# Sparse-coding kernel: coefficients scattered by index through DRAM in place of one-hot rows, sums and transposes

## The reference, cut to what matters

```python
D = dictionary / (norm(dictionary, axis=0) + EPS)      # 512 x 256
h_bar = (D.T @ X).T                                    # per patch: 256 scores
for k in range(1, 6):
    index = argmax(abs(h * ~mask))                     # one atom a step
    ...                                                # solve for x_stack (k coefficients)
    h = h_bar - einsum('bk,bkn->bn', x_stack, G[I])    # G = D.T @ D + eps
coeffs = zeros((B, N)).at[bidx[:, None], I].set(x_stack)
x = x1 + from_patches(D @ coeffs.T)
```

## Time and profile before

| | |
|---|---|
| median of 3 runs | 619.07 us (617.48 to 621.41) |
| the profiled execution | 618.9 us, of it 616.8 us from the first to the last instruction |
| VectorE busy | 523.9 us (85%) |
| TensorE busy | 459.3 us (74%) |
| ScalarE busy | 310.9 us (50%) |
| GpSimd busy | 222.6 us (36%) |
| mean granted TensorE clock | 0.902 of full speed |

### The profile page before, as it was taken

How to read it: one execution, slowest core, us unless ns; L and a number is a source line. 1 busy time by engine, 2 the same in 40 slices (tenths; PEclk the granted TensorE clock), 3 DMA queues, 4 the chain that set the end, 5 groups by cost and what they waited for, 6 DMA issues and landing times.

```text
span 616.8 us, 8489 instructions
## 1 busy us (share of the span) xinstructions
PE 459.3 (74%) x1778; PEld 321.4 (52%) x1778; DVE 523.9 (85%) x2507; ACT 310.9 (50%) x682; POOL 222.6 (36%) x269
## 2 busy tenths in 40 slices
PE   0198939895758588889985687889984456896955
PEld 0134925464657344567873354567962345674643
DVE  4492588989998899999977999999997999989980
ACT  3534564864662748656474397457222433552212
POOL 3000045343014645370033737450147364704440
PEclk9999978997879589989997699989996777999879
DMA  6979024994000367740202241121103211211113
GB/s 106 171 109 143 18 63 97 152 155 81 2 0 18 86 136 132 127 96 22 60 9 59 70 109 47 57 68 35 36 20 91 60 35 52 75 39 41 34 35 70
DMA packets 108190, 43.38 MB, mean 70 GB/s; under 512 B 103408, under 2 KB 103920, under 8 KB 108144
## 3 DMA queue, kind: packets, MB, share of 16 engines
q1 hardware_dynamic: 102000, 26.13, 25.1%
q0 software_dynamic: 6144, 16.79, 10.3%
HBM read 34.24 MB, written 8.65 MB: 70 GB/s over the span
## 4 chain that ended last, share of the span: by engine, by line
DVE 47%; PE 27%; issue 12%; SPq 4%; DMA 3%; ACT 3%; POOL 1%; DVEq 0%; ACTq 0%; another core or an unknown queue 0%; POOLq 0%
PE h L399 15%; DVE picked L1058 11%; DVE junk L968 9%; PE back_ps L399 9%; DVE top_i L916 7%; DVE junk L971 6%; DVE top L910 3%; SPq L250 3%; DMA rows<-gram,idx_u 2%; PE conv_ps L399 2%; ACT diag L641 1%; POOL rows L356 1%; ACT score L632 1%; DMA d_sb<-in_L_conv_dictionary 1%; SPq L257 1%
## 5 line engine op out<-in xcount | busy, mean ns | idle before, releaser
L399 PE MATMUL h<-rows,diag 128*128 128x256 f32 x640 | 175.4, 438 | 94.5 <-ACT diag L641 53.6
L399 PEld LDWEIGHTS h<-rows,diag 128*128 128x128 f32 x640 | 138.8, 221 | 134.1 <-DMA rows<-gram,idx_u 51.9
L356 POOL DMA_INDIRECT rows<-gram,idx_u x128 | 126.6, 989 | 223.4 <-DVEq L956 183.0
L370 POOL TENSOR_TENSOR picked<-picked 128x256 f32<-128x256 f32 x120 | 91.0, 763 | 150.7 <-DVEq L1062 134.5
L641 ACT ACTIVATE diag<-ident,dx 128x128 f32<-128x128 f32 x320 | 96.8, 388 | 67.5 <-DVEq L1045 52.6
L632 ACT ACTIVATE score<-h 128x512 f32<-128x512 f32 x80 | 47.4, 595 | 116.5 <-PE h L399 94.1
L910 DVE MAX8 top<-score 128x8 f32<-128x256 f32 x160 | 64.7, 415 | 27.3 <-issue 13.0
L1058 DVE TENSOR_SCALAR picked<-iota,idx_last,x_last 128x256 f32<-128x256 f32 x160 | 81.4, 545 | 2.4 <-DVE picked L1058 1.0
L971 DVE SCALAR_TENSOR_TENSOR junk<-mask,rows 128x256 bf16<-128x256 bf16 x224 | 82.6, 433 | 0.0
L399 PE MATMUL h<-d_sb,z 128*128 128x256 f32 x256 | 62.8, 407 | 8.3 <-DVEq L901 7.3
L399 PEld LDWEIGHTS h<-d_sb,z 128*128 128x128 f32 x256 | 61.0, 328 | 10.1 <-DVEq L901 7.0
(11 more groups left out here) (148 smaller groups left out, 586.0 us busy)
## 6 DMA issues: line engine op xcount, KB each, us to landing
xa<-in_x SPq DMA_DIRECT2D x64, 128.0 KB
out<-x SPq DMA_DIRECT2D x64, 128.0 KB
xb<-in_x SPq DMA_DIRECT2D x42, 128.0 KB
rows<-gram,idx_u POOLq DMA_INDIRECT x128
xb<-in_x SPq DMA_DIRECT2D x14, 120.0 KB
rows<-in_x SPq DMA_DIRECT2D x6, 128.0 KB, 4.4
d_sb<-in_L_conv_dictionary SPq DMA_DIRECT2D x4, 128.0 KB, 4.0
gram<-coef_t SPq DMA_DIRECT2D x1, 256.0 KB, 2.2
```

What stands on the lines that cost most here:

```text
L356: pool.indirect_dma_start(out=rows[s][:, k, t, :], out_offset=None, in_=gram_dram[:, :], in_offset=bass.IndirectOffsetOnAxis(ap=idx_u[s][: ...
L370: last = nc.gpsimd.tensor_tensor(picked[:, m % 2, t, 0, :], picked[:, m % 2, t, 0, :], picked[:, m % 2, t, j, :], ALU.add)
L399: return nc.tensor.matmul(dst, lhs, rhs, start=start, stop=stop, skip_group_check=skip)
```

## The change

A DRAM matrix `coef` of 16 images by 256 atoms by 256 patches is filled with zeros once, by one SyncE DMA ahead of the loads of round 1. At step 4 VectorE computes with two small operations the places of the 20 coefficients of each patch row (`place`), and `x_last` already negated. GpSimd scatters them with indirect DMAs, one for each tile and step (128 places of 4 bytes each), ten an image; SyncE loads the transposed matrix back into one of now four `coef_t` buffers (256 KB an image, `load_coef`). One-hot rows, sums, transposes and copies go, but for images 2 and 3 of the last round: their one-hot rows are made by VectorE at the very end (`spread`), summed and transposed by TensorE in PSUM (`coef_sums`) and copied by ScalarE. The last round is reconstructed in the order 0, 2, 3, 1. On TensorE `reconstruct(b, 0)` now stands behind `update(r, 1, 0)`, `reconstruct(b, 2)` behind `update(r, 1, 3)`, and `reconstruct(b, 3)` behind `correlate(f, 0)`; the `out_back`s on ScalarE move with them. Staging buffers at the start move to other tiles.

The diff, cut to its core:

```diff
+        coef_dram = nc.dram_tensor("coef", [IMAGES * ATOMS * 2 * P, 1], F32, kind="Internal").ap()
...
+            sp.wait_ge(pads_zero, 1)
+            sp.dma_start(coef_dram.rearrange("(i p n) a -> p i (n a)", p=P, n=CHUNKS * ATOMS),
+                         zeros.rearrange("p (a n) -> p a n", a=1).to_broadcast([P, IMAGES, CHUNKS * ATOMS])
+                         ).then_inc(zeros_stored, 16)
...
+            def load_coef(r, m):
+
                 n = IMG_R * r + m
+                sp.wait_ge(scattered[m], 16 * 2 * STEPS * (r + 1))
+                if not (isinstance(r, int) and r == 0):
+                    sp.wait_ge(recon_ps, 2 * (n - IMG_R) + 2)
...
+                sp.dma_start(coef_t[m][:, :, :], src).then_inc(coef_loaded[m], 16)
...
+                b = r - 1
+                if behind:
+                    load_coef(b, 0)
+                if front:
+                    load_ahead(r + 1, 0, more)
+                if behind:
+                    store(b, 0)
+                if front:
+                    load_ahead(r + 1, 1, more)
+                    load_ahead(r + 1, 2, more)
+                if behind:
+                    load_coef(b, 1)
+                if front:
+                    load_ahead(r + 1, 3, more)
+                if behind:
+                    store(b, 1)
+                    load_coef(b, 2)
+                    store(b, 2)
+                    load_coef(b, 3)
+                    store(b, 3)
...
+            def scatter(r, m, steps=range(STEPS), tiles=(0, 1)):
+
+                hold(pool, x_last_ready[m // 2], r + 1)
                 for t in tiles:
...
+                    for j in steps:
+                        pool.indirect_dma_start(out=coef_dram[:, :],
+                                                out_offset=bass.IndirectOffsetOnAxis(
+                                                    ap=place[m // 2][:, tile, j:j + 1], axis=0),
+                                                in_=x_last[m // 2][:, tile, j:j + 1], in_offset=None
+                                                ).then_inc(scattered[m], 16)
...
+                if behind:
+                    scatter(b, 3)
+                scatter(r, 0)
...
+            def coef_sums(m):
...
+                    for k in range(CHUNKS):
+                        for j in range(STEPS):
+                            last = mm(dst[:, k, t * P:(t + 1) * P], picked(tile, j)[:, k * P:(k + 1) * P], ident[:, :],
+                                      t == 0 and k == 0 and j == 0, j == STEPS - 1, True)
...
-                if behind:
-                    coef_transposes(b, 0)
-                    reconstruct(b, 0)
                 update(r, 0, 0)
                 update(r, 1, 0)
+                if behind:
+                    reconstruct(b, 0)
...
                 update(r, 0, 3)
-                if behind:
-                    coef_transposes(b, 2)
+                update(r, 1, 3)
+                if behind:
                     reconstruct(b, 2)
-                update(r, 1, 3)
-                if behind:
-                    coef_transposes(b, 3)
+                if front:
+                    correlate(f, 0)
+                if behind:
                     reconstruct(b, 3)
...
+                    if not (isinstance(r, int) and r == 0):
+                        for m in (2 * s, 2 * s + 1):
+                            hold(dve, scattered[m], 16 * 2 * STEPS * r)
...
-                    if k == STEPS - 1:
-                        rows_of = scatter(r, 0)
-                    select(r, 1, k, rows_of)
...
-                run(chain[1], rows_of)
-                if front:
-                    run(scatter(r, 1))
...
+                run(chain[1])
```

More of the change, by code:

```diff
@@ L317, in _ @@
             body(ROUNDS - 1, False, False, True)
-            for m in range(IMG_R):
-                store(ROUNDS - 1, m)
+            load_coef(ROUNDS - 1, 0)
+            load_coef(ROUNDS - 1, 1)
+            for position, m in enumerate(LAST_ORDER):
+                store(ROUNDS - 1, m, position)
             sp.wait_ge(y_stored, 16 * PATCH * IMAGES)
@@ L360, in _ @@
             pool.wait_ge(gram_stored, 16)
-            pool_base = n
-            def sum_picked(r, m, tiles=(0, 1), left_out=0):
+            pool.wait_ge(zeros_stored, 16)
+            def scatter(r, m, steps=range(STEPS), tiles=(0, 1)):
+                hold(pool, x_last_ready[m // 2], r + 1)
                 for t in tiles:
[L368 to L376, removed]
@@ L378, in body @@
-            def body(r, behind):
[L379 to L385, removed]
-            sums_after = {(1, 0): 1, (0, 2): 2, (0, 3): 3}
+                    tile = 2 * (m % 2) + t
+                    for j in steps:
[4 more added lines that the diff above has]
+                                                ).then_inc(scattered[m], 16)
@@ L504, in reconstruct @@
                     if q == 0:
-                        pe.wait_ge(coef_t_done, n + 1)
+                        if position is not None and m >= 2:
+                            pe.wait_ge(coef_t_done, m - 1)
+                        else:
+                            pe.wait_ge(coef_loaded[m], 16 * (r + 1))
                     for c2 in range(2):
                         for k in range(CHUNKS):
-                            last = mm(back_ps[half][:, c2, :], d_t[:, k, 2 * half + c2, :], coef_t[:, k, :], False,
+                            last = mm(back_ps[half][:, c2, :], d_t[:, k, 2 * half + c2, :], coef_t[m][:, k, :], False,
                                       k == CHUNKS - 1, True)
@@ L702, in body @@
                 diags(r, 0, 0)
-                if behind:
-                    out_back(b, 0)
                 if front:
@@ L712, in body @@
                 diags(r, 0, 1)
+                if behind:
+                    out_back(b, 0)
                 if front:
@@ L770, in _ @@
             body(ROUNDS - 1, False, True)
-            for m in range(IMG_R):
-                copy_coef(ROUNDS - 1, m, final_ps)
-                out_back(ROUNDS - 1, m)
+            copy_coef(2)
+            out_back(ROUNDS - 1, 0, 0)
+            copy_coef(3)
+            for position, m in enumerate(LAST_ORDER[1:], 1):
+                out_back(ROUNDS - 1, m, position)
         @block.vector
@@ L813, in _ @@
                 step(v.memset(xb_first[3 * C:4 * C, m, GR - 1, :], 0.0))
+            step(v.memset(zeros, 0.0))
             sync()
@@ L920, in scan, with select @@
                     pass
-            def select(r, s, k, other=iter(())):
+            def select(r, s, k, other=iter(()), on_chip=False):
                 sync()
@@ L1101, in _ @@
             dve.wait_ge(const_done, 1)
+            for m in range(1, IMG_R):
+                half = first_place[m // 2][:, 2 * (m % 2):2 * (m % 2) + 2]
+                step(v.tensor_scalar(half, half, float(m * ATOMS * 2 * P), None, ALU.add))
             run(variance(0, 0, x_stats_ps, x_var))
@@ L1170, in body @@
                 for k in range(STEPS):
-                    rows_of = scatter(r - 1, k + 1) if behind and k in (1, 2) else nothing
                     beside = [nothing] * 4
```

208 lines of the change are left out of this document (106 added, 102 removed).

## The result

The changed kernel took 674.4 us (median of 4, 667.7 to 680.9) against 618.9 for the kernel before: a ratio of 1.086 (95% interval 1.076 to 1.095). One of the four, 680.9, was more than 1.5% above the fastest and isn't in the ratio. The forecast was 610, range 600 to 622. It was wrong in size and in sign: the kernel got 55 us slower.

The account below looks back on a forecast made before the run. No single engine bounds it; without one-hot rows TensorE sets the pace, VectorE in round 3. 9 - 6.5 - 2 - 9 = -8.5 from a span of 616.8 gives 608.3, plus 2.1: 610 us, range 600 to 622 (own terms 603 to 619).

Parts of the forecast that it names:

- the one on GpSimd: GpSimd's issues: at 1.25 us a scatter, 90 us of issues in a round of 130, so hidden.
- Rival 3: Scatters dear on GpSimd: at 2.5 us each, gathers come late and GpSimd becomes the bound, about 655 us; chance 9%.
- The factor of five: GpSimd's DMA descriptors wait while VectorE holds the shared port: about 620 to 3100 ns, 40 scatters over 200 us a round.
- Zeros, +9: Start: the zeros' store on SyncE's queue delays round 1's loads and everything behind by 9 us (7.4 to 20.5).
- Round 0 into 1, -6.5: Without one-hot rows at round 0's end, `correlate(1, 1)` ends earlier and VectorE's `variance` runs 6.5 us earlier.
- Round 1, -2: End of round 1: VectorE saves 8 us, but 2 arrive, since `x_statistics` stand behind TensorE's reconstructions and `out_back(b, 3)`.
- Rounds 1 and 2, steps 0 to 3, nothing: The moved 7.2 us reconstruction fills TensorE's gaps; VectorE's savings turn into waits for scores, so no gain.
- GpSimd hidden: Each group of three to five scatters fits into the 9 to 11 us between two gathers, so gathers aren't late.
- Round 3 and the end, -9 and 0: Round 3 gains 9 us from selects, sums and a wait gone; the end, with four reconstructions behind VectorE, 0 within 3.
- 3 us: Loading back image 3's coefficients is due about 3 us before use, other images' 20 us or so.

Follow-up runs that it names:

- e1: The changed kernel without the scatters' DMAs, GpSimd only adding to the semaphore in their place; coefficients left out of the output: 616.4 us, ratio 0.995.
- i_after: The changed kernel itself, unchanged, run again in a set that records nearly all landings: 618.1 us, ratio 0.997.
- f2: The changed kernel without the scatters' DMAs and with the zeros stored behind the loads of round 1: 606.9 us, ratio 0.979.
- i_late: The changed kernel with all scatters, only the zeros stored behind the loads of round 1, in a set that records nearly all landings: 609.0 us, ratio 0.984.
- g_sp: f2's kernel with 40 more small DMAs a round issued by SyncE, in four runs of ten: 622.2 us.
- g_paced: f2's kernel with 16 more indirect DMAs a round, each behind a 128x512 addition on GpSimd: 666.2 us.
- g_run: f2's kernel with 16 more indirect DMAs a round in one run behind the last gather, read by nobody: 604.9 us.

## Why the prediction was wrong

**The step that failed is the one on GpSimd.** It priced a scatter by its issue alone, found GpSimd hidden, and put what scatters do to the other engines at nothing, without a reason. The whole sum took it that an update of a semaphore arrives when the work is done, beside any number of DMAs. In the sets that miss records that isn't so: 268 indirect DMAs instead of 128 cost 58 us (674.4 against e1's 616.4). That is the miss in size and sign. Why some sets hold updates up and others don't stays open.

Rival 3 had the right sign and the right place, GpSimd's DMAs. That its 655 lies near 674 is luck, because its mechanism was wrong: a scatter issues in 1.00 us, not 2.5, and GpSimd still mostly waits for VectorE ahead of its gathers (208 us in all, 183 before). Its 9% was too little for a kind of DMA that no row showed. The factor of five that the prediction took from the Trainium skill (SBUF — State Buffer, "A bandwidth-pool intuition that's wrong (but worth ruling out)") is not seen: the mean issue of a scatter is 1.00 us in the first set and in i_after.

The other steps are read in the trace of i_after, where nothing is held up, against the rows of before. That trace is of the shortest of ten executions (615.2 us, median 618.1). Its windows by round, and from VectorE's last `dx` to the end (as the earlier trace rows; DVE is the third busy time):

```profile
75.85:191.20 115.35, 84.28 (x341) 59.90 (x341) 100.13 (x559) 71.44 (x164) 41.97 (x42) 0.87 0.42 74
191.20:317.84 126.64, 105.75 (x412) 73.20 (x411) 100.52 (x560) 69.97 (x157) 71.46 (x73) 0.91 0.46 88
317.84:445.23 127.39, 105.69 (x415) 73.97 (x414) 100.65 (x559) 76.97 (x169) 71.73 (x72) 0.92 0.27 66
445.23:561.70 116.47, 82.55 (x284) 63.62 (x284) 97.53 (x531) 43.33 (x106) 71.00 (x72) 0.85 0.25 64
561.70:613.40 51.70, 44.34 (x194) 32.72 (x192) 7.04 (x20) 11.99 (x12) 10.14 (x11) 0.90 0.27 61
```

- **Zeros, +9: measured +7.2.** The store landed in 14.0 us (I took 14). ScalarE starts on the first load of round 1 at 53.8 instead of 48.2 and on the next image's at 68.6 instead of 61.4, and round 0 starts at 75.85 instead of 68.70, 7.2 us later (8.1 in the first set). That is just under the lower bound of 7.4. Moving the store off the path gave 9.5 us (f2 against e1) and 9.1 (i_late against i_after). The mechanism was right.
- **Round 0 into 1, -6.5: measured -4.5.** VectorE's `variance` of round 1 starts at 198.90 instead of 196.29, 2.6 us later, where the sum had 2.5. The agreement is luck, since two misses of 2 us cancel: the zeros cost less, and `correlate(1, 1)` started 0.4 us later than before on top of them (189.35), not 1.5 earlier. That `variance` waits for it, 3.8 us, was right.
- **Round 1, -2: measured -2.9.** The `variance` of round 2 starts at 329.5 (before 329.8); the forecast was 9 - 6.5 - 2, so 330.3. The mechanism is the one named: VectorE reaches round 2 early (317.84 against 326.03) and waits 7.8 us there, for TensorE's sums behind `x_statistics`:

```profile
DVE gn L892 <- PE conv_ps L455: 21.0, 5, 7.8
```

- **Rounds 1 and 2, steps 0 to 3, nothing: right.** In round 2 TensorE is idle for 1.8 us from the step-0 updates to the reconstruction of image 1 (346.96 to 395), and VectorE waits 6.5 us for scores at step 2, as the prediction had it. VectorE is busy 100.5 us a round (forecast 101).
- **GpSimd hidden: nearly.** The prediction would be wrong "if gathers start later behind scatters than behind sums", and they do. From VectorE's last write of the indices to a gather's first issue it is about 0.8 us where nothing stands between and at most 1.9 behind sums; in i_after it is up to 2.5 in round 2 and 3.9 in round 3. The gather of stream 0, step 3 in round 3, first the end of VectorE's indices, then GpSimd's last scatter and the first issue of the gather, without idle time between:

```profile
507.82 0.17 DVE L997 TENSOR_SCALAR idx_u<-best 128x4 uint32<-128x4 uint32 x1
```

```profile
510.51 1.08 POOL L416 DMA_INDIRECT coef<-x_last,place  x1 [0.30 <-issue]
511.89 1.10 POOL L402 DMA_INDIRECT rows<-gram,idx_u  x1 [0.30 <-issue]
```

  The chain that ended last runs over GpSimd's issues from 488.3 to 503.9 there, and TensorE then waits 3.5 us for rows. In all it is little: i_after is 1.7 us above e1 and i_late 2.1 above f2, the same kernels without scatters, though in other sets.
- **Round 3 and the end, -9 and 0**: measured -3.1 (613.4 - 616.8, less the 0.3 at the marker). Here lies the miss that is left, 6 us. VectorE's last `dx` comes at 561.3 instead of 585.1, a gain of 24, but the stretch behind it is 20 us longer (52.1 against 31.7): it belongs to TensorE, and TensorE isn't ready for it:

```profile
552.49 1.97 PE L455 MATMUL back_ps<-x,ident 128*128 128x256 f32 x4
560.09 3.78 PE L455 MATMUL back_ps<-coef_t,d_t 128*128 128x256 f32 x8 [5.63 <-DMA coef_t<-coef]
```

  SyncE's queue in that stretch:

```profile
553.89 2.61 SPq L323 DMA_DIRECT2D out<-x  x4
556.94 0.37 SPq L315 DMA_DIRECT2D coef_t<-coef  x1
```

  The scatters of image 3 were all issued by 541.6. Its load stands on SyncE behind `store(b, 2)`, which waits until ScalarE has written image 2 at 553.8. I had put this load at "3 us" ahead of its use and didn't ask what SyncE's queue held ahead of it. That is the 5.63 us above, and the next load costs 1.04 us in the same way. e1, without scatters, has the same two waits (6.3 us), so they aren't the scatters' own time. Both waits lie on the chain that ended last; that the time falls by as much once the loads stand ahead of the stores wasn't tried.
- **The sum**: 7.2 - 4.5 - 2.9 - 3.1, so -3.4 in the span with its rounding, against a forecast of -8.5. By medians it is -2.3 (618.1 against 620.4), and the time 618.1 against 610. The bounds of the terms, added as the prediction says, give about 601 to 621 (zeros at most 12), not 603 to 619.

So without the hold-up the change moves the kernel by -0.3%, within what can't be told from nothing, and with the zeros late by -1.6%. In the sets with the hold-up it is 7 to 9% slower (8.6% in the first), and 6.8% with the zeros late.

## What to carry to other kernels

A DMA issue that is hidden on GpSimd isn't free for that reason: count how many indirect DMAs a change adds, and where the trace has waits by an unknown releaser beside them, test with the same DMAs and no reader, on more than one chip. Before you read a cause out of such a trace, compare how complete its records are (is there a time to landing on the page?), and run one file in more than one set. And where a transfer moves onto a queue that works in order, ask what waits ahead of it there, not only when its data is ready.

## What the runs showed of the hardware that was not expected

- Up to 20 of GpSimd's indirect DMAs in a row (one in 1.25 us) leave the other engines alone in one set of runs (VectorE 24.05 us busy of 26) and hold them up in another (14.06 of 26), with one file.
- In the sets that hold up, no difference shows between such DMAs that read or write, or move 4 bytes or 1 KB a piece (683 us for reads of 4 bytes, 667 for writes of 1 KB, 668 to 681 for writes of 4 bytes; one execution of each of the first two).
- DMAs of 128 writes of 4 bytes to neighbouring words of DRAM are much dearer than to the places of the change, where only patches with the same atom share a row of 1 KB: 833.9 us (one execution) against 674.4, with 71 us of waits for loads.
- 160 small DMAs from SyncE's queue cost 15 us (g_sp against f2), without late updates.
- Additions on GpSimd slow VectorE where they alternate with GpSimd's DMAs: a masked extract takes 580 ns instead of 420 (g_paced, g_run).
